# Masked graph attention, three layers on 16 graphs: low weight parts made on GpSimd, and a prologue job table written in another order

## The reference

```python
def gnn_layer0(x, adj):                   # 16 graphs, 512 nodes, 256 features; two sub-layers k = 0, 1
    mask = adj == 0
    for k in range(2):
        q = x @ Wq[k].T + bq[k]           # 128 wide
        kk = x @ Wk[k].T + bk[k]
        scores = where(mask, -1e10, q @ kk.T / sqrt(128))
        attn = where(mask, 0, softmax(scores))
        x = layer_norm(x + (attn @ x) @ Wc[k].T, ln_g[k], ln_b[k])
    return x

def gnn_layer1(x, adj):                   # 8 heads of 32
    q, k, v = x @ Wq + bq, x @ Wk + bk, x @ Wv + bv
    scores = where(adj == 0, -inf, q_h @ k_h.T / sqrt(32))
    y = concat_h(softmax(scores) @ v_h) @ Wo + bo + x
    return layer_norm(y, gamma, beta)
```

## Time and profile before

| | |
|---|---|
| median of three runs | 1202.79 us (1202.02 to 1202.92) |
| the profiled execution | 1202.1 us, span 1200.0 us |
| TensorE busy | 1154.6 us, 96% of the span |
| VectorE, ScalarE, GpSimd busy | 982.9, 928.5, 530.9 us |
| waits of TensorE in the first 130 us | the longest 6.2 us |

### The profile page before, as it was taken

How to read it: one execution, slowest core, us unless ns; L and a number is a source line. 1 busy time by engine, 2 the same in 40 slices (tenths; PEclk the granted TensorE clock), 3 DMA queues, 4 the chain that set the end, 5 groups by cost and what they waited for, 6 DMA issues and landing times.

```text
span 1200.0 us, 28462 instructions
## 1 busy us (share of the span) xinstructions
PE 1154.6 (96%) x9596; PEld 843.5 (70%) x9596; DVE 982.9 (82%) x2688; ACT 928.5 (77%) x2115; POOL 530.9 (44%) x398
## 2 busy tenths in 40 slices
PE   7788999999999999999999999999999999999796
PEld 4566677777777777777777777777777777777463
DVE  5777788888888888888888888888888888988776
ACT  4426887888888788888878888887888888788774
POOL 1222445443564444356444534644453464444330
PEclk9898999999999999999999999999999999999999
DMA  8015160532517053251615325261432516122311
GB/s 228 19 36 141 20 190 24 148 81 73 140 37 194 19 141 90 72 141 36 180 33 136 89 72 148 36 179 34 127 89 80 148 36 180 34 71 72 111 32 36
DMA packets 164446, 112.48 MB, mean 94 GB/s; under 512 B 100944, under 2 KB 146000, under 8 KB 164304
## 3 DMA queue, kind: packets, MB, share of 16 engines
q1 hardware_dynamic: 162144, 102.80, 33.1%
q0 software_dynamic: 2160, 7.87, 1.9%
HBM read 61.87 MB, written 25.17 MB: 73 GB/s over the span
## 4 chain that ended last, share of the span: by engine, by line
PE 87%; DVE 6%; issue 2%; ACT 2%; DMA 2%; POOL 1%; DVEq 0%; SPq 0%; POOLq 0%; ACTq 0%
PE ps_j L848 39%; PE ps_t L861 22%; PE ps_j L988 9%; PE ps_s L840 8%; PE ps_s L834 6%; ACT probs L1048 1%; DMA xt<-ys 1%; DVE masked_s L1149 1%; PE ps_j L996 1%; POOL ys L674 1%; PE ps_j L955 0%; DVE wq L1199 0%; DVE y_l L1268 0%; DMA x<-x_dram 0%; DVE stats_L L1169 0%
## 5 line engine op out<-in xcount | busy, mean ns | idle before, releaser
L1149 DVE CUSTOM_DVE_ANT_0 masked_s<-ps_s,mask 128x512 f32<-128x512 f32 x640 | 424.6, 681 | 21.8 <-PE ps_s L840 20.7
L1048 ACT ACTIVATE probs<-masked_s,nm_h 128x512 f32<-128x512 f32 x512 | 367.3, 718 | 70.4 <-DVE nm_h L1149 63.9
L861 PE MATMUL ps_t<-ident,probs 128*128 128x128 f32 x2560 | 391.3, 276 | 5.6 <-ACT pt_h L1054 2.8
L861 PEld LDWEIGHTS ps_t<-ident,probs 128*128 128x128 f32 x2560 | 306.1, 142 | 85.5 <-issue 23.5
L1054 ACT ACTIVATE pt_h<-ps_t 128x512 f32<-128x512 f32 x401 | 236.2, 589 | 79.0 <-PE ps_t L861 74.3
L840 PE MATMUL ps_s<-stack 128*128 128x512 f16 x512 | 194.5, 380 | 2.6 <-DVE nm_h L1149 1.7
L848 PE MATMUL ps_j<-xw,pt_l 128*128 128x256 f16 x1536 | 189.1, 274 | 2.1 <-DVE xw L1294 2.1
L848 PEld LDWEIGHTS ps_j<-xw,pt_l 128*128 128x128 f16 x1536 | 151.0, 98 | 32.9 <-issue 2.2
L656 POOL TENSOR_TENSOR rstd_L<-var_eps_L,minus_half 128x4 f32<-128x4 f32 x32 | 32.8, 1024 | 246.5 <-DVE var_eps_L L1179 246.5
L988 PE MATMUL ps_j<-pt_h,v 128*32 128x256 f32 x2048 | 123.6, 382 | 2.4 <-DVE pt_h L1156 2.4
L1184 DVE TENSOR_TENSOR pt_l<-ps_t,pt_l 128x512 f16<-128x512 f32 x128 | 88.3, 690 | 32.5 <-ACT pt_l L1054 26.1
(11 more groups left out here) (140 smaller groups left out, 1639.4 us busy)
## 6 DMA issues: line engine op xcount, KB each, us to landing
stack<-bounce SPq DMA_DIRECT2D x256, 128.0 KB, 3.1
bounce<-parts SPq DMA_DIRECT2D x64, 256.0 KB, 2.6
adj_t<-adj_dram SPq DMA_DIRECT2D x30, 512.0 KB, 5.2
x<-x_dram SPq DMA_DIRECT2D x16, 512.0 KB, 3.9
out_dram<-y_f POOLq DMA_DIRECT2D x15, 512.0 KB, 3.4
stack<-adj_dram SPq DMA_DIRECT2D x2, 512.0 KB, 5.6
pt_h<-l_wc SPq DMA_DIRECT2D x2, 256.0 KB, 4.6
out_dram<-y_f SPq DMA_DIRECT2D x4, 128.0 KB, 1.8
```

What stands on the lines that cost most here:

```text
L861: last = pe.transpose(ps_t[r % 2][:, t], probs[:, r, t * P:(t + 1) * P], ident[:])
L1048: act.activation(probs[:, r], masked_s[:, r], ACT.Exp, bias=nm[:, n, r:r + 1], scale=-1.0, accum_out=total[:, n, r:r + 1]).then_inc(exps, 1)
L1149: dve.tensor_tensor_reduce(out=masked_s[:, r], in0=ps_s[scores_bank(pos)][:], in1=m[:, r], scale=-scale, scalar=NONE_LEFT, op0=ALU.add, op ...
```

## The change

Three things are done together, all in the prologue.

1. GpSimd makes four of the six low parts by a new function `low_weights(n, m)`: wc of sub-layer 1 and all three of the heads' layer. VectorE keeps wq and wk of sub-layer 1. Each is two scalings into a scratch (`y_f`) and one subtraction. TensorE waits on a semaphore of its own for them.
2. Job `B` uses bank 0 instead of 2 and comes at tile 4 of the first block instead of 5, as does `X` of graph 0's sub-layer 1; both, `W` of that sub-layer's second half and `XW` half 0 are prompt. The casts `W` of the heads' weights come at 5 instead of 7.
3. In the block of tiles 12 to 15, `X` of graph 0's final rows and the first half of the heads' q and k (`QH` 0, 0) are done ahead of the block's scores, and the rest of `QH` and `V` one tile sooner.

```diff
       ("XW", (1, 2), 1, 0, (3, 4)),
-      ("W", None, 0, 1, (3, 3, 7)),
-      ("X", (0, 1), 0, 1, (5, 5)),
-      ("B", (2,), 0, 0, (5,)),
-      ("QK", (0, 1), 0, 1, (6, 6)),
-      ("W", None, 0, 2, (7, None)),
-      ("AV", (2, 0), 1, 0, (7, None, None, None))]),
+      ("B", (0,), 0, 0, (4,)),
+      ("W", None, 0, 1, (3, 4)),
+      ("X", (1, 0), 0, 1, (4, 4)),
+      ("QK", (1, 0), 0, 1, (6, 6)),
+      ("W", None, 0, 2, (5, None)),
+      ("AV", (2, 1), 1, 0, (7, None, None, None))]),
...
-     [("QK", (0, 1), 1, 1), ("N", None, 0, 1), ("W", None, 0, 2, (1,)), ("XW", (2, 0), 1, 1)],
-     [("X", (1, 2), 0, 2, (0, 0)),
-      ("QH", (0, 1), 0, 0, (1, 1)),
-      ("QH", (2, 0), 0, 1, (2, 3)),
-      ("V", (1, 2), 0, 0, (3, 3)),
+     [("QK", (1, 0), 1, 1), ("N", None, 0, 1), ("XW", (2, 2), 1, 1, (0,)), ("X", (1, 0), 0, 2),
+      ("XW", (2, 2), 1, 1, (1,)), ("QH", (1, 0), 0, 0)],
+     [("QH", (2, 1), 0, 1, (1, 2)),
+      ("V", (0, 2), 0, 0, (2, 3)),
...
+            def low_weights(n, m):
+
+                full, part, width = split_weights[n][m]
+                up = y_f[:].rearrange("p t d -> p (t d)")[:, m % 2 * DC * D:m % 2 * DC * D + DC * width]
+                pool.wait_ge(scaled, 1)
+                pool.wait_ge(weights_hi, 3 + (3 * (n - 1) + m + 1) * DC)
+                settle(pool)
+                for c in range(DC):
+                    at = slice(c * width, (c + 1) * width)
+                    last = pool.tensor_scalar(up[:, at], full[:, at], gain_up[:, n - 1, c:c + 1], None, ALU.mult)
+                last.then_inc(weights_up, 1)
+                pool.wait_ge(weights_up, 1 if n == 1 else m + 2)
+                pool.tensor_tensor(part(1), up, part(0), ALU.subtract).then_inc(low_weights_ready, 1)
...
-            layer_norm_l0(0, 0, x1)
+            split_y(0, 0)
+            pool.wait_ge(weights_ready, 1)
+            low_weights(1, 2)
+            gain_and_shift("L", nth(0, 0), y_l, 0, x1)
+            low_weights(2, 0)
+            low_weights(2, 1)
 
             split_y(1, 0)
-            split_y(0, 1)
-            pool.wait_ge(weights_ready, 3)
+            low_weights(2, 2)
+            pool.wait_ge(low_weights_ready, 4)
             pool.tensor_tensor(y_f[:], y_turn, gain[:, 0:1, :].to_broadcast([P, NT, D]), ALU.mult)\
                 .then_inc(gained["L"], 1)
+            split_y(0, 1)
```

More of the change, by code:

```diff
@@ L65 @@
       ("XW", (1, 2), 1, 0, (3, 4)),
-      ("W", None, 0, 1, (3, 3, 7)),
-      ("X", (0, 1), 0, 1, (5, 5)),
-      ("B", (2,), 0, 0, (5,)),
-      ("QK", (0, 1), 0, 1, (6, 6)),
-      ("W", None, 0, 2, (7, None)),
-      ("AV", (2, 0), 1, 0, (7, None, None, None))]),
+      ("B", (0,), 0, 0, (4,)),
[4 more added lines that the diff above has]
+      ("AV", (2, 1), 1, 0, (7, None, None, None))]),
     (3, [("L", 1, 0)],
      [],
-     [("AV", (2, 0), 1, 0, (None, 0, 1, 2)),
+     [("AV", (2, 1), 1, 0, (None, 0, 1, 2)),
+      ("XW", (0, 2), 0, 1, (2, 3)),
       ("N", None, 1, 0, (3,)),
-      ("XW", (1, 2), 0, 1, (2, 3)),
-      ("Z", (0,), 0, 0, (3,)),
-      ("AV", (1, 2), 0, 1, (3, 3, 3, 3))]),
+      ("Z", (1,), 0, 0, (3,)),
+      ("AV", (0, 2), 0, 1, (3, 3, 3, 3))]),
     (3, [("L", 1, 1)],
-     [("QK", (0, 1), 1, 1), ("N", None, 0, 1), ("W", None, 0, 2, (1,)), ("XW", (2, 0), 1, 1)],
-     [("X", (1, 2), 0, 2, (0, 0)),
-      ("QH", (0, 1), 0, 0, (1, 1)),
-      ("QH", (2, 0), 0, 1, (2, 3)),
-      ("V", (1, 2), 0, 0, (3, 3)),
+     [("QK", (1, 0), 1, 1), ("N", None, 0, 1), ("XW", (2, 2), 1, 1, (0,)), ("X", (1, 0), 0, 2),
+      ("XW", (2, 2), 1, 1, (1,)), ("QH", (1, 0), 0, 0)],
+     [("QH", (2, 1), 0, 1, (1, 2)),
+      ("V", (0, 2), 0, 0, (2, 3)),
       ("AV", (1, 2), 1, 1, (3, 3, None, None))]),
@@ L111 @@
 PROMPT = {("QK", 1, 0, 0), ("QK", 1, 0, 1), ("W", 0, 1, 0), ("AV", 0, 0, 2), ("AV", 0, 0, 3), ("X", 0, 1, 0),
-          ("X", 0, 1, 1), ("QK", 0, 1, 0), ("QK", 0, 1, 1), ("AV", 1, 0, 2), ("AV", 1, 0, 3), ("X", 0, 2, 0),
-          ("X", 0, 2, 1), ("QH", 0, 0, 0), ("QH", 0, 0, 1)}
+          ("X", 0, 1, 1), ("QK", 0, 1, 0), ("QK", 0, 1, 1), ("AV", 1, 0, 2), ("AV", 1, 0, 3), ("B", 0, 0, 0),
+          ("W", 0, 1, 1), ("XW", 0, 1, 0)}
 PARTS = {"AV": 4, "OG": 3, "R": 1, "N": 1, "S": 1, "B": 1, "Z": 1, "U": 1, "C": 1, "D": 1, "M": 1}
@@ L276, in graph_attention @@
         floors_in = sem("floors_in")
+        weights_up, low_weights_ready = sem("weights_up"), sem("low_weights_ready")
         waits_passed = sem("waits_passed")
@@ L948, in job @@
                         pe.wait_ge(bias_ready, 1)
-                        pe.wait_ge(weights_ready, 2)
+                        pe.wait_ge(low_weights_ready, 1)
                     for t in range(2):
@@ L961, in job @@
                         pe.wait_ge(weights_in, 16 * N_WEIGHTS_IN)
-                        pe.wait_ge(weights_ready, 3)
+                        pe.wait_ge(low_weights_ready, 4)
                     out_bank = bank(banks[half], before)
@@ L1257, in job @@
                     dve.wait_ge(scaled, 1)
-                    low_weights(l, range(3) if l == 2 else ((0, 1), (2,))[half - 1])
+                    low_weights(l, (0, 1))
                 if name == "M":
```

## The result

The changed kernel takes 1194.87 us (median of 4 runs, 1193.67 to 1195.64), the kernel before on the same chips 1202.4 (4 runs, 1201.62 to 1202.92): ratio 0.9938, 95% interval 0.9926 to 0.995. That is 7.5 us won; 5.3 were forecast, and the range of 1194.3 to 1200.4 held the time, 0.6 us from its lower end. The profiled execution took 1193.67 us, its span is 1191.8.

A forecast was written before the change was run, and what follows sets the result against it. Bound: TensorE, 87% of the chain, with a 6.2 us hole at job B in the prologue. 6.7 - 1.0 - 0.7 + 0.3 = 5.3 us won gave 1197.5 us, range 1194.3 to 1200.4.

The forecast's parts named there:

- The hole at B: TensorE stands 6.2 us at job B for XW's low part; with B early, tile 8's mask comes 6.7 sooner.
- the collision: VectorE's low-part pair on wq takes 4.6 us beside GpSimd's 2.34 us products; kept apart, wk's pace, 0.6 for two.
- The low parts on GpSimd: Four low parts move to GpSimd, 2.3 us a round, bound 2.7, with 8 us of cover: cost nothing.
- GpSimd late: Rival, chance 0.05: TensorE or the turning DMA waits for GpSimd's low parts; slower, 1205 at 10 us a round.
- The clock: TensorE's 1.9 us lull ahead of tile 8's scores halves its clock: 1.0 us lost, bounds 0 and 2.
- Tiles 8 to 15: Tile 8's transposes to row sums: QK 1.8 longer behind the DMA lull, tile 12's mask 6.0 later; 0.7 lost.
- the bound of 1.1: Favourable bound for the stretch of tiles 8 to 15: 1.1 us won if the clock never falls.
- The sum: Whole prologue: 6.7 - 1.0 - 0.7 = 5.0, plus 0.3 for overlapping clock losses: 5.3 us won.
- the clock never falls in the new lulls: Rival, chance 0.15: TensorE keeps its full clock behind the prologue's new lulls; 7.8 us won, 1195.0.
- the reordered block gives it all back: Rival, chance 0.10: X and QH ahead of the scores make tile 12 6.0 later, tail keeps 16.0; no change, 1203.

The follow-up runs named there:

- e1: The kernel before with one wait added, so GpSimd's product for x1 starts behind VectorE's low parts: 1198.03 us against 1202.21.
- e10: The changed kernel with GpSimd's product and sum for x1 put back ahead of its first low part: 1198.45 us against 1202.28, ratio 0.9967.
- e2: The kernel before with only GpSimd's four low parts and their waits, job tables otherwise as before: 1194.18 us against 1202.21.
- e9: The changed kernel with every scaling of a GpSimd low part done three times, each behind the one before: ratio 0.9992 to the kernel before.
- e5: The changed kernel, unaltered, run again on another chip: 1193.52 us, ratio 0.9937 to the kernel before.
- e4: The changed kernel with the block of tiles 12 to 15 back in its old order: 1193.49 us against 1202.21 for the kernel before.
- e6: e4 with N of graph 1 put ahead of the rest of XW: 1191.02 us, ratio 0.991 to the kernel before.
- e7: e4 with the first half of the casts of the heads' weights at tile 7 instead of 5: 1190.41 us, ratio 0.9905 to the kernel before.
- e8: e4 with the edits of both e6 and e7: 1189.37 us, ratio 0.9899 to the kernel before.
- e12: The changed kernel, new block of tiles 12 to 15 included, with the edits of both e6 and e7: 1191.76 us against 1202.59, ratio 0.9909.
- e3: The kernel before with only the block of tiles 12 to 15 in the new order: 1205.56 us against 1202.21.

## Why the prediction was right, and where its sizes were off

*The hole at B, and the collision: right.* The pair on wq was to fall to the pace of wk; it takes 0.61. QK of graph 0's second sub-layer was forecast for 42.5 and the chain has it at 42.05 (42.9 with the earlier start put back). Tile 8's mask was forecast 6.7 sooner and is 6.45. e1 and e10 show from both sides that the overlap is worth 3.5 to 4.2 us. What the prediction's bookkeeping hid is shown by e2: the prediction credited most of the 6.7 to the new order, but e2 wins 8.0 us without it.

*The low parts on GpSimd: right that they are free, wrong in size.* A round takes 3.05 us; 2.3 was taken and 2.7 given as the bound. The step that failed is the price of the scaling, 0.55 to 0.76 us from the rows with two scalars; it is 0.91. The cover was put at 8 us and was 6.1 at the power, 7.5 at N. Neither cost anything. e9 bears out the step's own warning, each us beyond the cover moves the DMA by one (12.3 - 7.5 = 4.8), but not all that the lateness costs: 2.0 of its 6.8 us are the slower DMA and the clock. It also shows a wrong count in the rival "GpSimd late", which puts two rounds in front of graph 1's power and so the point where it decides at 9 us a round: three stand there, and at 7.1 us a round the gain was gone (ratio 0.9992).

*The clock: the term that was too large.* 1.0 us was charged behind the lull ahead of tile 8 and 1.8 behind the DMA; neither was paid there. In the changed kernel's trace the lull ahead of tile 8 isn't even there, since the clock had fallen at 40 us already and QK at half speed filled it. In e5, the same program, it is there (TensorE waits 1.89 us for k) and the clock stays. Behind the DMA lull, 2.1 us instead of 3.6, it stays too. The clock did fall in new places, at 40 and at 64 (in e5 only the second, at 62.6), but there its price was covered: by ScalarE's casts at the first, all but 0.8 us, and by the DMA at the second. TensorE's windows (start:end, us, busy, granted clock), changed kernel and then e5:

```profile
40.00:46.00 6.00, 5.06 (x14) 0.50 0.01 3
46.00:48.00 2.00, 2.00 (x14) 0.83 0.00 0
48.00:62.00 14.00, 14.00 (x115) 1.00 0.01 2
...
64.00:66.00 2.00, 2.00 (x11) 0.50 0.00 0
66.00:68.00 2.00, 2.00 (x15) 0.71 0.00 0
68.00:100.00 32.00, 25.19 (x169) 1.00 0.45 127
```

```profile
40.00:46.00 6.00, 5.02 (x33) 1.00 0.02 4
46.00:48.00 2.00, 0.14 (x1) 1.00 0.00 0
48.00:62.00 14.00, 13.24 (x108) 1.00 0.00 1
```

Two executions of one program, and the six us at half clock cost 0.79 us at tile 8 (49.81 against 49.02). So 0.8 us did go to the clock ahead of tile 8, but before the place where it was charged and in one of two executions only, and the 6.45 already hold it: without it, in e5, tile 8's mask is 7.27 sooner. That 6.45 comes so close to the forecast 6.7 is in part luck.

*Tiles 8 to 15: the direction right, the sum on the other side of nothing.* Tile 12's mask was forecast 6.0 later against tile 8's than before and is 4.0 later (34.71 us behind it instead of 30.67); 1.8 of the missing 2 is the half clock that wasn't there. The stretch from tile 12's transposes to the row sums was forecast to shrink from 16.0 to 10.8 and is 11.3. Together 0.7 was to be lost and 0.7 is won (48.30 us from tile 8's mask to the row sums before, 47.59 now), inside the bound of 1.1.

*The sum:* forecast 6.7 - 1.0 - 0.7 + 0.3 = 5.3; in the trace 6.45 + 0.71 = 7.16, and 0.86 of luck at the start; by the medians 7.5. It ended nearest to the rival "the clock never falls in the new lulls", 7.8 won, and as far as the two lulls it names go (the one ahead of tile 8 and the one before the DMA) that rival is what happened. The 5.3 lay inside the range, but the 1.8 charged behind the DMA was never paid. The rival "the reordered block gives it all back" had the right mechanism in half of its size: part 3 lengthens one stretch by what it takes off the next, and alone it makes the kernel slower, but not by the 5.7 that it would have needed.

## What to carry to other kernels

When an operation is several times slower than its twin, look at what the other engine of the pair was doing in just that time: one wait, which orders GpSimd's 2.3 us products behind four VectorE operations of 0.3 us, won 4.2 us and cost nothing. A reordering that brings work forward pays only up to the next thing that comes at its own pace, here a turning DMA; so first move what starts that DMA, and split the lull ahead of it so that the clock falls, if it does, on work that nobody waits for. Time the parts of a change one by one: here part 1 alone gave all of the gain, part 2, worth 3.1 alone, gave no more than 0.7 on top of it, and part 3 nothing.

## What the runs showed of the hardware

- The granted clock can fall behind gaps under 1 us: in the changed kernel it is at half from 40 us on, behind gaps of TensorE of 0.59 and 0.45 us and just ahead of one of 0.95, and a lull of 1.9 us (e5, e4) left it at full. Of eight profiled executions with the same work up to 40 us, e4, e5, e6 and e7 kept the full clock there, the changed kernel, e8, e9 and e12 did not (e9 had it back at 43 us, the other three between 46 and 47). What decides was not tried.
- The very first mask starts between 17.07 and 18.02 us in the fourteen traces, with the same instructions up to there. By tile 8 two executions of one program can be 0.8 us apart (changed kernel and e5), two of equal work 1.3 (before and e3): a difference of under 1 us between single traces says nothing by itself.
- GpSimd's scaling of 128x256 fp32 by one scalar a partition, from one tile to another, takes 0.91 us; with two scalars and in place it is 0.55.
- VectorE's small SBUF operations are held by GpSimd too, but not all: 128x2 (L1267) took 1.01 us beside a cast of GpSimd and 128x4 (L1198) 0.79 beside a product, where each takes 0.15 to 0.17 elsewhere, while four of 128x1 (two of them with an input in PSUM) took 0.14 to 0.15 beside a product in e10. The changed kernel's timeline, 64 and 72 us:

```profile
64.29 1.01 DVE L1267 TENSOR_SCALAR bk<-bk 128x2 f32<-128x2 f32 x1
...
72.19 0.79 DVE L1198 TENSOR_SCALAR minus_mean_L<-moments_L 128x4 f32<-128x4 f32 x1
```
